# A transformer layer on one core: every engine's order of items is written anew, and the spread of the values goes in four parts

## What is computed

```
x = x + attn(moe(x, cond_64))      # mixture of 8 experts + 1 shared, banded linear attention, layer norm
c = cond2_attention(x, null_kv=cond_64)
x = x + ffn(c)
# cond2: xn = ln(x); q = xn @ Wq (16 heads of 64); k, v = xn @ Wkv, one null key in front;
#        q, k l2-normed; sim = q k^T * 8 + relative position bias, causal; softmax; @ v; @ Wout; ln
# ffn:   h = silu(x w1) * (x w2); h = gelu(h h1); h = gelu(h h2); h @ w3
```

## Time and profile before

| what | value |
|---|---|
| median of 3 runs (lowest to highest) | 832.1 us (830.48 to 832.76) |
| the profiled execution | 828.2 us, of it a span of 826.5 us |
| busy: PE, DVE, ACT, POOL | 87%, 70%, 63%, 43% |
| mean granted clock of PE | 0.946 |
| period of a steady iteration (from spread to spread on SP) | 92.3 us |
| DMA | 27.31 MB, mean 33 GB/s |

### The profile page before, as it was taken

How to read it: one execution, slowest core, us unless ns; L and a number is a source line. 1 busy time by engine, 2 the same in 40 slices (tenths; PEclk the granted TensorE clock), 3 DMA queues, 4 the chain that set the end, 5 groups by cost and what they waited for, 6 DMA issues and landing times. The chain is left out here.

```text
span 826.5 us, 18078 instructions
## 1 busy us (share of the span) xinstructions
...
## 2 busy tenths in 40 slices
...
DMA packets 47786, 27.31 MB, mean 33 GB/s; under 512 B 22592, under 2 KB 45264, under 8 KB 47312
## 3 DMA queue, kind: packets, MB, share of 16 engines
q1 hardware_dynamic: 47392, 26.15, 11.3%
...
q10 hardware_dynamic: 304, 0.01, 0.0%
...
## 5 line engine op out<-in xcount | busy, mean ns | idle before, releaser
L701 POOL TENSOR_TENSOR sb_sm<-sb_sm,sb_rden 128x128 f32<-128x128 f32 (+3 forms) x128 | 97.1, 764 | 230.5 <-DVE sb_rden L1177 230.4
L800 ACT ACTIVATE sb_sm<-sb_sm,sb_nmx 128x65 f32<-128x65 f32 (+3 forms) x512 | 178.2, 352 | 16.5 <-DVE sb_nmx L1173 16.1
L1166 DVE SCALAR_TENSOR_TENSOR sb_sm<-ps_S,sb_rq,sb_biasm 128x65 f32<-128x65 f32 (+3 forms) x512 | 112.2, 292 | 9.6 <-PE ps_S L1416 8.0
L683 POOL TENSOR_TENSOR sb_rq<-sb_qss,sb_mhalf 128x16 f32<-128x16 f32 x32 | 93.6, 2947 | 53.9 <-DVE sb_qss L1150 53.9
L693 POOL TENSOR_TENSOR sb_biasm<-sb_bias,sb_maskn 128x128 f32<-128x128 f32 (+3 forms) x128 | 109.1, 871 | 15.9 <-DVE sb_sm L1166 11.8
L800 ACT ACTIVATION_READ_ACCUMULATOR sb_sm<-sb_sm,sb_nmx 128x1 f32 x512 | 96.6, 189 | 0.0
L1294 PE MATMUL ps_M<-sb_xh,sb_wguh 128*128 128x512 f32 x78 | 39.0, 500 | 58.8 <-DVE sb_xl L1050 57.0
L1440 PE MATMUL ps_S<-sb_pT,sb_vblk 64*128 64x128 f32 (+1 forms) x896 | 83.3, 329 | 6.5 <-DVE sb_pT L1189 6.1
L1440 PEld LDWEIGHTS ps_S<-sb_pT,sb_vblk 64*128 64x128 f32 x896 | 70.1, 188 | 25.3 <-issue 11.1
L1453 PEld LDWEIGHTS ps_z<-sb_wout,sb_oT 128*128 128x128 f32 x512 | 62.9, 192 | 9.5 <-issue 6.0
L1453 PE MATMUL ps_z<-sb_wout,sb_oT 128*128 128x128 f32 x512 | 67.4, 279 | 0.0
...
## 6 DMA issues: line engine op xcount, KB each, us to landing
...
sb_vblk<-sb_vs SPq DMA_DIRECT2D x128, 32.0 KB, 1.9
...
sb_qs<-in_xT SPq DMA_DIRECT2D x1, 2048.0 KB, 10.8
...
```

What stands on the lines that cost most here:

```text
L683: pool.tensor_tensor(rq[:, cut], qss[:, cut], mhalf[:], ALU.pow).then_inc(q_rnorm.sem, 1)
L701: pool.tensor_tensor(p, p, stat(rden, g, j).unsqueeze(2).broadcast_to([128, 4, wide - 1]), ALU.mult)\
L800: ins = act.activation(p[:, t], p[:, t], ACT.Exp, bias=least[:, t:t + 1], accum_out=total[:, t:t + 1])
L1166: ins = dve.scalar_tensor_tensor(scored(g, j)[:, t], bank(g, "sim", n, odd)[:, first:first + wide], rq[:, col:col + 1], masked_bias(j % 4) ...
```

## The change

Two parts of the program differ. First, `spread_values` issues four of its 16 DMAs per call, and SP's order calls it as `vb.0` to `vb.3`. Each call repeats the waits. Second, nearly every order in `ORDER` is written anew. Each engine still has the same items in each kind of iteration. The core of the diff (PE, ACT, DVE and POOL have 6 orders each; shown are those that the prediction speaks of):

```diff
     "pe fill": """
-        lg.0 warm.0-5 lg.1-6 pb.0 rw.0 lg.7 pb.1 exp.0-4 down.0 pb.2 warm.6 qkv.0 scores.0 pb.3 warm.7 mix.0
-        warm.8-11 fl.0 warm.12-13 fl.1-2 warm.14 wr.0 warm.15 xnT.0 warm.16-17 q.0-1 kv.0 q.2-4 qs.0-3 q.5-7
-        kT.0 qs.4-7 warm.18-21
+        lg.0 warm.0 lg.1-2 pb.0 lg.3 pb.1 lg.4 warm.1 lg.5-7 rw.0 exp.0 pb.2 exp.1 pb.3 exp.2-4 down.0 qkv.0
+        scores.0 warm.2 mix.0 warm.3-7 fl.0 warm.8-9 fl.1-2 warm.10-13 wr.0 warm.14 xnT.0 warm.15 kv.0 q.0-2
+        warm.16 q.3-4 qs.0-3 q.5-7 warm.17 qs.4-7 kT.0 warm.18-21
     "pe start": """
-        sim.0-1 rw.0 exp.0-2 sim.2-3 exp.3-4 down.0 sim.4 qkv.0 scores.0 sim.5 mix.0 PV.0-1 sim.6 z.0 PV.2-3
-        xnT.0 z.1 sim.7 q.0-1 z.2 q.2 PV.4 kv.0 q.3 z.3 q.4 qs.0-3 PV.5 q.5 PV.6 q.6 PV.7 q.7 kT.0 qs.4-7 z.4-7
+        sim.0-1 rw.0 sim.2-3 exp.0-4 down.0 sim.4 PV.0 qkv.0 scores.0 sim.5 mix.0 PV.1 sim.6 z.0-1 PV.2-3 z.2
+        sim.7 z.3 xnT.0 PV.4 kv.0 PV.5 q.0 PV.6 q.1 PV.7 kT.0 q.2-3 qs.0-1 z.4 q.4-6 qs.2-3 q.7 qs.4-7 z.5-7
     "pe steady": """
-        sim.0-1 exp.0-4 down.0 sim.2 zT.0 sim.3 qkv.0 l1.0 sim.4 l1.1 PV.0 l1.2-3 scores.0 PV.1 sim.5 l2.0-3
-        mix.0 z.0 l3.0-2 sim.6-7 xnT.0 l3.3 z.1 kv.0 q.0-1 PV.2-4 q.2-3 l4.0 q.4 z.2 PV.5 qs.0-3 PV.6-7 z.3
-        q.5-7 z.4 kT.0 qs.4-7 z.5-7
+        sim.0-2 exp.0-4 down.0 zT.0 sim.3-4 qkv.0 l1.0 PV.0 l1.1-2 PV.1 l1.3 scores.0 l2.0-1 sim.5 l2.2 mix.0
+        l2.3 sim.6-7 l3.0-1 z.0-1 l3.2 xnT.0 l3.3 q.0 kv.0 l4.0 PV.2-7 q.1-3 z.2 q.4-5 qs.0-3 q.6 z.3 q.7 z.4
+        qs.4-7 z.5 kT.0 z.6-7
     "act steady": """
-        xh.0 exp.0-4 ex.0-2 down.0 zT.0 ex.3 qkv.0 l1.0-1 h1.0-1 l1.2-3 h1.2 ex.4 h1.3 ex.5-6 PV.0 ex.7 l2.0-1
-        h2.0 l2.2 h2.1 l2.3 h2.2-3 ex.8-9 l3.0-1 PV.1 ex.10 xnT.0 l3.2-3 ex.11-12 q.0-1 ex.13 PV.2 q.2 PV.3
-        ex.14-15 q.3 PV.4 q.4-6 PV.5 q.7 kT.0 PV.6-7
+        xh.0 exp.0-4 ex.0-2 down.0 zT.0 ex.3 qkv.0 ex.4 l1.0-1 h1.0-1 l1.2-3 h1.2-3 ex.5-7 l2.0-1 h2.0-1 PV.0
+        l2.2 PV.1 h2.2 l2.3 h2.3 ex.8-11 l3.0-2 xnT.0 l3.3 q.0 ex.12-15 PV.2-3 q.1-2 PV.4 q.3-7 PV.5-7 kT.0
     "dve start": """
-        rw.0 xl.0 sim.0 max.0 exp.0 sim.1 exp.1 max.1 exp.2 inv.0 pl.4 max.2-3 exp.3 inv.1-2 sim.2 tp.0 max.4
+        pl.4 sim.0 rw.0 max.0 sim.1 max.1 inv.0 max.2 xl.0 max.3 inv.1 exp.0 tp.0 exp.1 sim.2 exp.2 max.4-5
...
     "dve steady": """
-        xl.0 ln3.0 sim.0 exp.0 max.0 exp.1-3 max.1 sim.1 exp.4 max.2 zT.0 inv.0-1 down.0 max.3 zl.0 sim.2 inv.2
...
-        max.14 q.2 inv.13 max.15 kT.0 tp.10-12 inv.14 tp.13 l4.0 vs.0 tp.14 inv.15 tp.15 q.3-6 ssq.0 ssc.0 q.7
+        ln3.0 sim.0 xl.0 sim.1 max.0 exp.0-3 max.1 exp.4 zT.0 max.2 sim.2 max.3 down.0 inv.0-1 max.4 inv.2 zl.0
...
+        q.0 kT.0 inv.13-14 tp.10-12 inv.15 tp.13-15 l4.0 vs.0 q.1-7 ssq.0 ssc.0
     "pool steady": """
-        zT.0 pn.0 bias.4-6 pn.1 bias.7-8 pn.2 bias.9 pn.3-4 bias.10-11 pn.5-6 xb.0 pn.7 bias.12 ln1.0 bias.13
-        ln2.0 pn.8-9 bias.14-15 pn.10 kv.0 pn.11 bias+.0 pn.12 bias+.1-3 pn.13-15 qn.0-3
+        bias.4 zT.0 bias.5-7 pn.0-2 bias.8 pn.3 xb.0 pn.4 bias.9 pn.5 bias.10 pn.6 bias.11-12 ln1.0 bias.13 pn.7
+        bias.14-15 ln2.0 pn.8 bias+.0 pn.9-10 bias+.1 kv.0 bias+.2 pn.11-15 bias+.3 qn.0-3
     "sp fill": """
-        vb.0 maskn.0 rw.0 hw.0 wr.0
+        wr.0 hw.0 vb.0 rw.0 vb.1-3 maskn.0
     "sp start": """
-        maskn.0 rw.0 hw.1 vb.0 wb.0
+        rw.0 hw.1 maskn.0 wb.0 vb.0-3
     "sp steady": """
-        rw.0 maskn.0 wb.0 l4.0 vb.0
+        rw.0 maskn.0 wb.0 l4.0 vb.0-3
     "sp seventh": """
-        maskn.0 rw.0 vb.0
+        rw.0 maskn.0 vb.0-3
@@ -584,15 +583,14 @@
-            def spread_values(g, k):
+            def spread_values(g, i):
                 sp.wait_ge(v_shifted.sem, v_shifted.at(g, 1))
                 if g == 0:
                     sp.wait_ge(v_cleared, 1)
                 sp.wait_ge(pv_psum.sem, pv_psum.at(g, 0))
-                for i in range(4):
-                    for c in range(4):
+                for c in range(4):
```

More of the change, by code:

```diff
@@ L75 @@
-        kv.0 q.0-1 z.0 sim.6 PV.2-3 sim.7 l2.3 z.1 q.2-3 l3.0 q.4 qs.0-3 q.5 l3.1 q.6-7 PV.4 qs.4-7 z.2-3 PV.5-7
-        z.4-5 kT.0 z.6-7
+        sim.0-2 exp.0-4 down.0 sim.3 zT.0 sim.4 qkv.0 l1.0 scores.0 PV.0 l1.1-2 sim.5 l1.3 PV.1 mix.0 l2.0-2 z.0
+        l2.3 xnT.0 sim.6 PV.2-3 kv.0 q.0-1 sim.7 z.1 q.2-3 z.2 q.4 z.3 qs.0-3 PV.4 q.5-6 l3.0 q.7 l3.1 qs.4-7
+        PV.5-7 z.4-5 kT.0 z.6-7
     """,
     "pe last": """
-        sim.0-1 l3p.2-3 sim.2 zT.0 l4p.0 l1.0 sim.3-4 l1.1-3 PV.0-1 sim.5 l2.0-2 z.0-1 l2.3 sim.6 PV.2-3 l3.0-1
@@ L113 @@
-        pb.3 exp.4 rt.6-7 down.0 rt.8 qkv.0 scores.0 mix.0 rt.9 ln1.0 pl.1-2 ln2.0 nk.1 xnT.0 q.0-1 kv.0 q.2-3
-        kT.0 vs.0 q.4-7 ssq.0 ssc.0 pl.3
+        cg.0 rt.0 pb.0 wl.0 pb.1 rt.1-3 pb.2 rt.4 rw.0 x0.0 pb.3 rt.5 exp.0-3 rt.6 pl.0 exp.4 xl.0 rt.7 down.0
+        rt.8 qkv.0 pl.1 scores.0 nk.0 mix.0 rt.9 ln1.0 ln2.0 pl.2 xnT.0 kv.0 q.0-1 kT.0 vs.0 maskn.0 q.2-3 pl.3
+        q.4 nk.1 q.5 ssq.0 ssc.0 q.6-7
     """,
     "dve start": """
-        rw.0 xl.0 sim.0 max.0 exp.0 sim.1 exp.1 max.1 exp.2 inv.0 pl.4 max.2-3 exp.3 inv.1-2 sim.2 tp.0 max.4
@@ L122 @@
+        exp.3 inv.2 tp.1 exp.4 sim.3 inv.3 pl.5 max.6 down.0 inv.4-5 tp.2-3 max.7 sim.4 inv.6 qkv.0 max.8
+        scores.0 inv.7 tp.4-6 max.9 inv.8 mix.0 sim.5 tp.7 inv.9 max.10 ln1.0 max.11 sim.6 ln2.0 max.12 tp.8-9
+        max.13 sim.7 inv.10-11 max.14 xnT.0 inv.12-13 max.15 tp.10-11 inv.14 tp.12-13 inv.15 kv.0 tp.14-15 q.0
+        kT.0 vs.0 q.1-2 maskn.0 q.3-7 ssq.0 ssc.0
     """,
     "dve steady": """
-        xl.0 ln3.0 sim.0 exp.0 max.0 exp.1-3 max.1 sim.1 exp.4 max.2 zT.0 inv.0-1 down.0 max.3 zl.0 sim.2 inv.2
@@ L129 @@
+        tp.0-1 inv.3 sim.3 max.5 qkv.0 l1.0 tp.2-3 l1.1 h1.0-1 l1.2 inv.4 max.6 l1.3 h1.2-3 scores.0 sim.4 tp.4
+        inv.5 max.7 tp.5 inv.6 sim.5 inv.7 h2.0 max.8 mix.0 tp.6 h2.1 max.9-10 h2.2-3 ln1.0 inv.8 max.11 tp.7
+        inv.9 sim.6 max.12 ln2.0 tp.8 maskn.0 inv.10 tp.9 xnT.0 max.13 inv.11 sim.7 max.14 kv.0 max.15 inv.12
+        q.0 kT.0 inv.13-14 tp.10-12 inv.15 tp.13-15 l4.0 vs.0 q.1-7 ssq.0 ssc.0
     """,
     "dve seventh": """
-        xl.0 ln3.0 sim.0 exp.0-3 max.0 sim.1 max.1-3 exp.4 sim.2 zT.0 down.0 inv.0-1 zl.0 tp.0 max.4 inv.2 max.5
```

65 lines of the change are left out of this document (31 added, 34 removed).

## The result

The changed kernel takes 762.9 us (median of 4 runs, 758.9 to 766.7), beside it the kernel before took 832.4 us (830.5 to 833.8): a ratio of 0.9166, 95% interval 0.911 to 0.922. The prediction was 784.1 us with a range from 772 to 812, so the direction was right and the gain, 69.5 us where 48.0 was predicted, lies beyond the range. The profiled execution took 765.0 us (span 763.3), 63.2 less than that of before (828.2).

A forecast was written before the change was run, and what follows sets the result against it. PE bounds the steady iterations and a latency chain the borders, with 57.0 us of waits for xl. Gains 8 + 11.8 + 21.2 + 7.0 = 48.0 (fill, into it1, four steady borders, into it6): 832.1 - 48.0 = 784.1 us, range 772 to 812.

The forecast's parts named there:

- The mechanism at the borders: Steady borders: more PE work behind PV.7 cuts the wait from 5.6 to 1.8 us; with clock, 21.2 over four.
- the SP chain: Between groups: from PV.7 through SP's 16 spread copies, x load and split to exp.0, 15.7 us.
- Into it1: Border into it1: 12.6 us of work behind PV.7 against a 15.7 chain; wait 3.1, not 14.9, gain 11.8.
- A: Rival: at group ends the softmax takes x's place, PV.7 waits for DVE's last turn; 818 us, chance 0.10.
- C: Rival, slower: ACT's ex.8-11 block holds the bank PE's xnT needs, up to 11.3 us a group; 852, chance 0.05.
- B: Rival: x really is requested before the spread, so SP's 10.8 us leave every chain; 777 us, chance 0.03.
- value 0: Inside the steady iterations: PE's 2.3 us of waits per group are left unchanged, gain 0.
- from below: Inside the iterations, one bound of the estimate: all waits vanish, 14 us gained in six groups.
- Last and drain 0, plus or minus 2: Iterations last and drain: little idleness to give, so 0, plus or minus 2 us.
- Fill: Border into it0: xnT 4.5, kv and vs 1.5, SP 1.7 + 2.3, less about 2; gain 8 us.
- kv and vs: Fill, DVE: kv.0 goes ahead of q.0-1 and vs.0 ahead of q.2-3, gain 1.5 us.
- SP's two moves: Fill: hw.0, wr.0 and mask leave between spread and load, 1.7 us; hw.0 out of x load's way, 2.3.

The follow-up runs named there:

- e7: Kernel after, PE's steady order alone changed: q.1-4 and z.2 between PV.4 and PV.5, so less work stands behind PV.7; 791.6 us, ratio 0.951.
- e2: Kernel after with the load of the next group's x truly ahead of the spread copies on SP; 760.8 us, ratio 0.917.
- e1: Kernel before with the x load moved ahead of the 16 spread copies on SP, all else unchanged; 781.1 us, ratio 0.940.
- e8: Kernel after, steady iterations: DVE's mask ahead of sim.6 and two GpSimd biases ahead of pn.9-10, so GpSimd works beside ln2; 783.3 us, ratio 0.942.
- e10: Kernel after with the orders of last and drain of before; 762.95 us.
- e6: Kernel after with SP's orders of before, all other engines as after; 782.6 us, ratio 0.941.

## Why the prediction was right or wrong

**The mechanism at the borders was right.** PE's work behind PV.7 hides the SP chain (e7), the rest is DVE's sim.0 (e2), and the wait was 1.7 us where 1.8 was predicted; from PV.7 to exp.0 it took 17.3 us, predicted 16.8. For the borders of it1 to it5 the sum had 20.7 us of waits and 7.5 of clock; they came as 21.0 and 7.0. One step of this chain was off without cost: PE was to wait for `xl` and sim.2 to hide in it, but it was sim.2 that waited, and `xl` was ready at 415.33, 0.4 us before exp.0. (The sum's own figures, 16.6 less 15.0, give 1.6.) Into it1, 11.8 was predicted and 13.0 came: PE waited 1.74 us, again for sim.0, and not 3.1 for `xl`, as its work behind PV.7 was 15.1 us and not 12.6. (The eight qs in it took 3.7 us, priced at 0.25 each, so 2.0.) This mis-sized term had put the limit on SP's chain instead of sim.0, and cost the forecast these 1.2 us. The split of `vb` changed nothing on SP, as said: the words of the change come true only where an experiment moves the load (first in e1). Of the rivals, A and C did not come: PE's wait for turned probabilities left the steady iterations, and none for ACT's gelu took its place. B is about the cause, not the size: its 777 is a time that after beats without doing what B says.

**The step that failed is "value 0" inside the iterations.** The end "from below" came true: both waits, 1.5 and 0.8 us in a steady iteration, vanished, and with them 10.6 us of idleness in it1 to it5; the difference between the measured 38.6 and the predicted 28.2 is 10.4. That was the largest miss. By itself it would have left the time at 773.7, inside the range; the other stretches (4.8 more together) bring it to 768.9, and the last 6 are the base (below). The rows to see it were in the trace of before: ln2 took 3.05 us there for what takes 1.1 in fill. I had priced ln2 by its place and never asked why it was slow.

The Trainium skill (SBUF — State Buffer, "Who interferes with whom") has the rule: `tensor_scalar` from SBUF to SBUF can enter a mode that takes both ports, and then it and GpSimd block each other, while one issued earlier wins. The times agree, in after 1.11 us alone and in e8 2.93 beside GpSimd; which mode an instruction took is in no trace. The prediction had used the same page against `xl`, where once more it didn't show: `xl` took 0.69 us in after amid 11.51 us of `qn`. For another operation with two SBUF inputs it did show. It took 0.69 us with GpSimd idle (before) and 1.39 beside GpSimd's addition (after; the last line is GpSimd's):

```profile
502.06 0.69 DVE L1096 TENSOR_TENSOR sb_x<-sb_hT,sb_xs 128x512 f32<-128x512 f32 x1
...
375.21 1.39 DVE L1094 TENSOR_TENSOR sb_x<-sb_hT,sb_xs 128x512 f32<-128x512 f32 x1
...
374.53 1.52 POOL L691 TENSOR_TENSOR sb_biasm<-sb_bias,sb_maskn 128x384 f32<-128x384 f32 x1
```

**"Last and drain 0, plus or minus 2" was right.** They gave 1.7 (e10). The other 5.1 of the 6.9 behind exp.0 of it6 (186.0 before, 180.9 in e10) are 1.1 of idleness inside the seventh, for which the sum had nothing, and 4.0 of busy time: about 1.5 by sim.1-2, which crossed the mark, and the rest by the clock behind the border, of which the sum had 1.5 in its 7.0 for this border.

**Fill was over-estimated, 4.7 for 8.** The table came 9.0 us earlier (its store at 43.10, before 52.09), where 10 was estimated, and PE's wait for it went. But xnT came at 65.09, 3.4 earlier and not 4.5, as a wait of 2.85 for ln2 took its place. DVE's kv.0, put first, then waited for PE, and the spread began only 2.6 earlier, so that the 1.5 of "kv and vs" became a loss of 0.8. Behind the wait the clock was low, which it had not been before (after, then before):

```profile
69.00:73.00 4.00, 4.00 (x13) 3.37 (x13) 2.46 (x5) 0.74 (x2) 0.92 (x1) 0.50 0.59 236
...
69.00:73.00 4.00, 3.21 (x23) 2.79 (x21) 1.39 (x2) 2.13 (x5) 2.65 (x3) 1.00 0.01 2
```

SP's two moves came nearly as priced: the load stood 0.04 us behind the spread, not 1.66, and landed 3.6 us after its issue, not 5.6. From landing to exp.0 it took 1.2 longer, as DVE and ACT now have other work first (2 predicted). So the load came 3.9 earlier and exp.0 4.7. What the prediction didn't see is that these moves are not an extra gain but what the other orders need: taken back alone they cost 10 us here (e6), since the new start orders wait for h first.

**The clock.** 1.5 us a border was right in size: between e10 and after, the same orders and waits differ by 1.0 and 2.7 us in the two periods with a lower clock. The prediction said that a pause of 1.8 us should not lower it. It did at two of six borders in after, and at none of six in e10.

**The base.** The sum of 48.0 was to be held against the traces' 63.2. The other 6 us are the distance of either profiled execution from its median: 2 by the clock in after; what made the 4 of before stays open.
